# Two attention stages read 64-row operands in place of zero-padded copies, and a third stage's PSUM banks and waits are rearranged

## What is computed

```python
def attn_a(x):                       # 16 heads of 64
    Q, K, V = heads(x @ Wq.T + bq), heads(x @ Wk.T + bk), heads(x @ Wv.T + bv)
    attn = sin(30.0 * (Q @ K.T) / 8)             # no softmax: 2048 x 2048 per head
    return concat(attn @ V) @ Wo.T + bo
def ffn(x):                          # two layers
    for l in range(2):
        q, k, v = split(shift_token(x) @ wqkv[l])          # 8 heads of 64
        q, k = rotary(l2norm(q)), rotary(l2norm(k))
        x = x + softmax(mask(8 * q @ k.T)) @ v @ wo[l]       # window 512: 1 to 5 blocks of 128 keys
        a, g = split(layernorm(shift_token(x)) @ w1[l] + b1[l])
        x = x + (a * gelu(g)) @ w2[l] + b2[l]
    return x
def attn_b(e):                       # two iterations
    for _ in range(2):
        q, k, v = e @ Wq.T, e @ Wk.T, e @ Wv.T             # 16 heads: keys of 16, values of 64
        res = e + softmax(q @ k.T / 4) @ v @ Wp.T
        e = res + relu(res @ W1.T + b1) @ W2.T + b2
    return e
x = x + attn_a(layernorm(x)); x = x + ffn(layernorm(x))
x = x + attn_b(layernorm(x)); x = x + ffn(layernorm(x))
```

## Time and profile before

| | us |
|---|---|
| three runs, median | 35545.85 |
| lowest and highest | 35491.78 and 35622.54 |
| the profiled execution | 35539.34 |
| its span on the slowest core, first to last instruction | 35537.5 |
| TensorE busy on it | 14172.3 (40%) |
| VectorE busy | 8219.3 (23%) |
| ScalarE busy | 6572.5 (18%) |
| mean granted TensorE clock on it | 0.61 of full speed |

### The profile page before, as it was taken

The page is one execution under the profiler, slowest core; times in us unless marked ns, Lnnn a source line. Parts: engine busy times, 40 slices in busy tenths (PEclk is TensorE's granted clock), DMA queues, the critical chain, the costliest instruction groups (busy, mean ns, idle before and its releaser), DMA issues.

```text
span 35537.5 us, 273198 instructions; the slowest of 8 cores (35410.4 to 35537.5 us)
## 1 busy us (share of the span) xinstructions
PE 14172.3 (40%) x81984; PEld 6048.0 (17%) x81984; DVE 8219.3 (23%) x17364; ACT 6572.5 (18%) x8716; POOL 604.9 (2%) x1083
## 2 busy tenths in 40 slices
PE   4555422532532453352333333332253253245235
PEld 1010111211111111121212122221121111111112
DVE  1010033133223213311111111113313322321331
ACT  1313212012002002102323132321201200210210
POOL 0000000000000000000000000000000000000000
PEclk7575555765665675575555555555576576557557
DMA  1010101110120120121010100000111012012012
GB/s 20 0 38 0 31 19 32 35 34 28 37 64 1 47 51 2 37 63 33 13 19 18 39 15 18 13 31 21 32 35 34 27 37 65 1 44 54 2 36 62
DMA packets 618568, 1055.36 MB, mean 30 GB/s; under 512 B 162154, under 2 KB 375395, under 8 KB 617156
## 3 DMA queue, kind: packets, MB, share of 16 engines
q1 hardware_dynamic: 265252, 710.02, 6.0%
q0 software_dynamic: 351904, 327.86, 5.7%
HBM read 987.54 MB, written 301.99 MB: 36 GB/s over the span
## 4 chain that ended last, share of the span: by engine, by line
PE 37%; DVE 21%; ACT 15%; DMA 13%; issue 11%; SPq 1%; DVEq 1%; ACTq 1%; POOL 0%; POOLq 0%
PE ps L901 6%; ACT pool L1204 5%; DMA pool<-zs 5%; PE ps L907 4%; PE ps L951 3%; PE ps L1220 3%; ACT pool L417 3%; DMA pool<-f_w1p 3%; PE ps L402 3%; PE ps L617 3%; ACT pool L755 2%; DMA pool<-xs 2%; DVE pool L748 2%; PE ps L1188 2%; PE ps L794 2%
## 5 line engine op out<-in xcount | busy, mean ns | idle before, releaser
L901 PE MATMUL ps<-pool 128*128 128x512 bf16 x5632 | 2061.2, 533 | 2300.7 <-DMA pool<-f_w1p 1232.7
L951 PE MATMUL ps<-pool 128*128 128x512 bf16 x5632 | 1827.0, 491 | 1411.1 <-DVE pool L974 777.3
L794 PE MATMUL ps<-pool 128*64 128x128 bf16 x4480 | 661.6, 307 | 4260.0 <-ACT pool L786 2249.9
L1204 ACT ACTIVATE pool<-ps 128x2048 bf16<-128x2048 f32 x1024 | 1922.1, 1877 | 2303.6 <-PE ps L1188 2303.5
L253 PE MATMUL ps<-pool 128*128 128x128 bf16 x3328 | 483.6, 299 | 3872.8 <-DMA pool<-zs 1737.7
L1220 PE MATMUL ps<-pool 128*128 128x65 bf16 x16384 | 1063.9, 243 | 2386.9 <-ACT pool L1204 2386.9
L913 ACT ACTIVATE pool<-ps,pool 128x512 f32<-128x512 f32 x704 | 483.8, 687 | 6807.9 <-PE ps L907 6807.8
L917 DVE TENSOR_SCALAR pool<-ps,pool 128x512 f32<-128x512 f32 x704 | 528.4, 751 | 4755.4 <-PE ps L907 4755.4
L907 PE MATMUL ps<-pool 128*128 128x512 bf16 x5632 | 1618.7, 439 | 0.0
L417 ACT ACTIVATE pool<-ps 128x1024 bf16<-128x1024 f32 x1024 | 1048.6, 1024 | 2047.2 <-PE ps L402 2047.2
L755 ACT ACTIVATE pool<-ps,pool 128x640 bf16<-128x640 f32 (+4 forms) x1024 | 744.9, 727 | 3663.7 <-DVE pool L751 3663.7
(11 more groups left out here) (155 smaller groups left out, 17823.8 us busy)
## 6 DMA issues: line engine op xcount, KB each, us to landing
zs<-pool SPq DMA_DIRECT2D x448, 512.0 KB
pool<-zs SPq DMA_DIRECT2D x448, 512.0 KB
pool<-xs SPq DMA_DIRECT2D x192, 512.0 KB
pool<-f_w1p POOLq DMA_DIRECT2D x176, 512.0 KB, 5.9
pool<-zs POOLq DMA_DIRECT2D x312, 256.0 KB, 3.3
xs<-pool SPq DMA_DIRECT2D x96, 512.0 KB
pool<-f_w2p POOLq DMA_DIRECT2D x16, 2816.0 KB, 17.8
pool<-x SPq DMA_DIRECT2D x64, 512.0 KB
```

The costliest lines, as they stand in the source:

```text
L794: first=(ji == 0), last=(ji == nk - 1): e.matmul(PS(5)[0:64, 0:128], vaug[:, 520*kc + 65*h: 520*kc + 65*h + 64], ptb[:, 640*pslot + 128*ji ...
L901: p.op("T", lambda e, kc=kc, tg=tg, abank=abank, w1b=w1b: e.matmul(PS(abank), w1b[:, 256*kc:256*kc+128], hlnFr()[:, kc, 512*tg:512*(tg+1)] ...
L951: last=(ci == nch - 1 and hhalf == 0): e.matmul(PS(bank), ohalf[:, 2048*ci + 128*t: 2048*ci + 128*(t+1)], w2buf[:, 1024*ci + 512*half: 102 ...
L1204: p.op("S", lambda e, eslot=eslot: e.activation(expS[:, 2048*eslot:2048*(eslot+1)], PS(0, 4), AF.Exp), waits=w, inc=sC)
```

## The change

Three parts, in the diff below. In the first attention `kf2`, its zeros, its copies and the wait on them go, and each of the two score matmuls contracts over the 64 partitions on which its head lies: K and Q are read in place, the first head from partitions 0 to 63, the second from 64 to 127. In the local attention `qp2` goes in the same way; the score matmuls of a head read `qpk` and `kpk` on the head's 64 partitions. In the second attention the value slots lie seven, seven and two to a bank; the transposes of the tail, the W1 output and the W2 outputs all go through bank 7; the join on TensorE ahead of W1 is replaced by a wait for VectorE on the first W1 matmul; and the first score matmul of every group but the first waits only for the previous group's last exponential and for VectorE's last copy out of bank 3. The first value matmul of each group also waits for the output projection's last add.

```diff
--- before.py
+++ after.py
@@ -371,43 +371,25 @@
             out=wvo[:].rearrange("p (c k) -> p c k", k=1024),
             in_=io["aWoT"][:].rearrange("(c p) k -> p c k", p=128)),
             waits=[(vC, vC.n)])
-        kf2 = mem.at("a_kf2", [128, 2 * 2048], BF16, mem.offs["a_xt"][0] + 8192)
-        p.op("G", lambda e: e.memset(kf2[64:128, 0:2048], 0.0),
-             waits=[(sC, sC.n), (vC, vC.n)])
-        p.op("G", lambda e: e.memset(kf2[0:64, 2048:4096], 0.0), inc=gC)
-        kzero = gC.n
-        kf2_done, s_last = {}, {}
         sin_done, av_done = {}, {}
         for hp in range(8):
-            wcp = [(vC, vC.n)] if hp == 0 else [(tC, s_last[hp-1])]
-            if hp == 0:
-                wcp.append((gC, kzero))
-            p.op("V", lambda e, hp=hp: e.tensor_copy(
-                kf2[0:64, 0:2048], KF[0:64, 2048*hp:2048*(hp+1)]), waits=wcp)
-            p.op("V", lambda e, hp=hp: e.tensor_copy(
-                kf2[64:128, 2048:4096], KF[64:128, 2048*hp:2048*(hp+1)]), inc=vC)
-            kf2_done[hp] = vC.n
             for qg in range(4):
                 for kc in range(16):
                     par = kc % 2
                     for which in range(2):
                         bank = 2 * par + which
+                        base = 64 * which
                         w = ([(sC, sin_done[(hp, qg, kc - 2)])]
                              if (hp, qg, kc - 2) in sin_done else [])
                         if kc == 0 and which == 0 and (hp, qg) == (0, 0):
                             w = [(sC, sC.n)]
-                        if kc == 0 and which == 0 and qg == 0:
-                            w = list(w) + [(vC, kf2_done[hp])]
-                        p.op("T", lambda e, hp=hp, qg=qg, kc=kc, bank=bank,
-                             which=which: e.matmul(
+                        p.op("T", lambda e, hp=hp, qg=qg, kc=kc, bank=bank, base=base: e.matmul(
                             PS(bank),
-                            kf2[:, 2048*which + 128*kc: 2048*which + 128*(kc+1)],
-                            QF[:, 2048*hp + 512*qg: 2048*hp + 512*(qg+1)],
+                            KF[base:base+64, 2048*hp + 128*kc: 2048*hp + 128*(kc+1)],
+                            QF[base:base+64, 2048*hp + 512*qg: 2048*hp + 512*(qg+1)],
                             start=True, stop=True), waits=w)
                     p.grp("T", tC)
                     smm = tC.n
-                    if qg == 3 and kc == 15:
-                        s_last[hp] = smm
                     slot = par
                     w = [(tC, smm)]
                     if (hp, qg, kc - 2) in av_done:
@@ -502,7 +484,6 @@
     zupd_off = mem.mark() - 2 * 1024 * 4
     scr = mem.seq("f_scr", [128, 1024], F32)
     nrm = mem.seq("f_nrm", [128, 128], F32)
-    qp2 = mem.seq("f_qp2", [128, 2 * 2048], BF16)
     oF = mem.at("f_oF", [128, 4 * 2048], BF16, hF_off)
     hlnF = mem.at("fB_hlnF", [128, 8 * 2048], BF16, hF_off)
     ohalf = mem.at("fB_ohalf", [128, 11 * 2048], BF16, kpk_off)
@@ -521,12 +502,6 @@
     tbr = lambda ti: tabs[:, 1024*ti:1024*(ti+1)].rearrange("p (t k) -> p t k", k=64)
 
     final_phase = dst is not zs and dst is not None
-
-    p.op("G", lambda e: e.memset(qp2[64:128, 0:2048], 0.0),
-         waits=[(sC, sC.n), (vC, vC.n)])
-    p.op("G", lambda e: e.memset(qp2[0:64, 2048:4096], 0.0), inc=gC)
-    qp2_zero = gC.n
-    qp2_war = {0: 0, 1: 0}
 
     for b in range(B_LOC):
         zwr, ln_s = {}, {}
@@ -697,14 +672,6 @@
 
             for h in range(8):
                 hb, hc2 = 64 * (h % 2), h // 2
-                hs = h % 2
-                wcp = [(sC, sC.n), (tC, qp2_war[hs])]
-                if h == 0 and b == 0:
-                    wcp.append((gC, qp2_zero))
-                p.op("V", lambda e, hb=hb, hc2=hc2, hs=hs: e.tensor_copy(
-                    qp2[hb:hb+64, 2048*hs:2048*(hs+1)],
-                    qpk[hb:hb+64, 2048*hc2:2048*(hc2+1)]), waits=wcp, inc=vC)
-                qp2_done = vC.n
                 prev_exp = 0
                 state = {}
                 ptev_hist = {-1: (vC, 0)}
@@ -720,14 +687,12 @@
                     st_ = state[qc] = dict(kcs=kcs, nk=nk, W_=W_, sb0=sb0, pslot=pslot,
                                            stat=stat)
                     w = [(sC, state[qc-2]["exp"])] if qc >= 2 else [(sC, sC.n)]
-                    if qc == 0:
-                        w = list(w) + [(vC, qp2_done)]
                     for ji, kc in enumerate(kcs):
-                        p.op("T", lambda e, hs=hs, hc2=hc2, qc=qc, kc=kc, ji=ji,
+                        p.op("T", lambda e, hb=hb, hc2=hc2, qc=qc, kc=kc, ji=ji,
                              sb0=sb0: e.matmul(
                             PS(sb0, 2)[:, 128*ji:128*(ji+1)],
-                            qp2[:, 2048*hs + 128*qc: 2048*hs + 128*(qc+1)],
-                            kpk[:, 2048*hc2 + 128*kc: 2048*hc2 + 128*(kc+1)],
+                            qpk[hb:hb+64, 2048*hc2 + 128*qc: 2048*hc2 + 128*(qc+1)],
+                            kpk[hb:hb+64, 2048*hc2 + 128*kc: 2048*hc2 + 128*(kc+1)],
                             start=True, stop=True),
                             waits=(w if ji == 0 else []))
                         p.grp("T", tC)
@@ -810,7 +775,6 @@
                     if qc >= 1:
                         emit_tail(qc - 1)
                 emit_tail(NT - 1)
-                qp2_war[hs] = state[NT - 1]["smm"]
             p.join(["T"], [vC, sC])
 
             ldwo = p.dma("G", lambda e, layer=layer: e.dma_start(
@@ -1166,10 +1130,12 @@
             PSF = PS(0, 8)
 
             def AVAP(i):
-                off = 512 * (4 + i // 6) + 65 * (i % 6)
+                off = 512 * (4 + i // 7) + 65 * (i % 7)
                 return PSF[:, off:off + 65]
             av_war = vC.n
             prev_av_last = tC.n
+            exp15_prev = sC.n
+            wp_v_prev = vC.n
             ptv_hist = {}
             bank_tok = {3: (vC, 0), 7: (vC, 0)}
             for ng in range(4):
@@ -1179,8 +1145,12 @@
                     avd = {}
                     exp_done = {}
                     for mg in range(16):
-                        w = ([(sC, exp_done[mg - 1])] if mg >= 1
-                             else [(sC, sC.n), (vC, vC.n)])
+                        if mg >= 1:
+                            w = [(sC, exp_done[mg - 1])]
+                        elif gcg == 0:
+                            w = [(sC, sC.n), (vC, vC.n)]
+                        else:
+                            w = [(sC, exp15_prev), bank_tok[3]]
                         for j in range(4):
                             for s in range(4):
                                 cc = 32 * ((s + j) % 4)
@@ -1212,11 +1182,12 @@
                                 if i == 0:
                                     w = [(sC, exp_done[mg])]
                                     if mg == 0:
-                                        w += [(gC, vones), (vC, av_war)]
+                                        w += [(gC, vones), (vC, av_war),
+                                              (vC, wp_v_prev)]
                                 p.op("T", lambda e, i=i, s=s, qq=qq, mg=mg, cg=cg,
                                      eslot=eslot,
-                                     first=(mg == 0 and i in (0, 6, 12)),
-                                     last=(mg == 15 and i in (5, 11, 15)):
+                                     first=(mg == 0 and i in (0, 7, 14)),
+                                     last=(mg == 15 and i in (6, 13, 15)):
                                      e.matmul(
                                     AVAP(i),
                                     expS[:, 2048*eslot + 512*s + 128*qq:
@@ -1227,8 +1198,9 @@
                         p.grp("T", tC)
                         avd[mg] = tC.n
                     av_last = prev_av_last = avd[15]
+                    exp15_prev = exp_done[15]
                     for jb in range(3):
-                        nsl = (6, 6, 4)[jb]
+                        nsl = (7, 7, 2)[jb]
                         p.op("V", lambda e, jb=jb, nsl=nsl: e.reciprocal(
                             scr[:, 8*jb:8*jb+nsl].rearrange("p (g k) -> p g k", k=1),
                             PSF[:, 512*(4+jb):512*(4+jb) + 65*nsl].rearrange(
@@ -1241,8 +1213,8 @@
                             w = [(vC, rcv), (tC, ptv_hist.get(gcg - 2, 0))]
                         p.op("V", lambda e, i=i, obslot=obslot: e.tensor_scalar_mul(
                             obf[:, obslot + 64*i: obslot + 64*(i+1)],
-                            AVAP(i)[:, 0:64], scr[:, 8*(i//6) + (i % 6):
-                                                  8*(i//6) + (i % 6) + 1]), waits=w)
+                            AVAP(i)[:, 0:64], scr[:, 8*(i//7) + (i % 7):
+                                                  8*(i//7) + (i % 7) + 1]), waits=w)
                     nrmv = vC.n
                     av_war = nrmv
                     for s in range(4):
@@ -1297,7 +1269,7 @@
```

(14 more changed lines are left out.)

## The result

Eight executions of each kernel gave a median of 34877.94 us (34840.6 to 34980.03) for the changed kernel and 35524.63 us (35475.63 to 35622.54) for the one before: ratio 0.982, 95% interval 0.9806 to 0.9835, 647 us faster. The forecast was 34960 us, 1.6% faster; the measured time lies within its range, 28 us above its lower end.

A forecast was written before the change was run, and what follows sets the result against it. No engine is full, so waits from engine to engine bound the kernel. Terms of 405, 37, 9, 72, 15, 33 and 12 us sum to 583 us, giving 34960 us, 1.6% faster, range 34850 to 35260.

The forecast's parts named there:

- The chain: Whole kernel: no engine is full, time is a chain of waits; in the first attention every part is on the path.
- Score pairs, 405 us: First attention: two half-row score matmuls overlap like the value pair, gaining 404.8 us over 1024 steps.
- The gap of 0.17 us: First attention, ahead of each score pair: put down to reshaping the array between kinds of matmul, expected to stay.
- the upper bound: First attention: the score pair also loses the gap in front of it, 174 us more; chance 0.03.
- Copies and zeros, 37 and 9 us: First attention: head-pair boundaries become ordinary steps, 37 us; less TensorE idle at the loop's start, 9 us.
- Local attention, 72 us: Changes of head: without the Q copy the mask add starts 1.28 us earlier, 56 times, 72 us.
- the slower rival: Local attention scores on one half: weight loads exposed, 35405 to 35412 us or 36131; chance 0.06, half of it slower.
- the slack: Local attention: transposes have 3.06 us of slack, hiding a 0.17 us drain after the scores; without it 174 us.
- Second attention, 15 + 33 + 12 us: Earlier scores at 48 group boundaries, 15 us; join ahead of W1, 33 us; scores after a tail, 12 us.
- the added wait: Second attention, first value matmul: waits for an add long past, looked at while the exponential runs; no cost priced.
- The sum: Whole kernel: 405 + 37 + 9 + 72 + 15 + 33 + 12 = 583 us gained.

The follow-up runs named there:

- same_half: Changed kernel with both score matmuls of the first attention on partitions 0 to 63, sharing one half of the rows: 35248.19 us, one execution.
- full_rows: Changed kernel with first-attention score matmuls over all 128 partitions of K and Q in place, no copies or zeros: 35240.49 us, one execution.
- av_wait_last: Changed kernel with the exponential's wait listed last of four at a group's first value matmul in the second attention: 34808.9 us, one execution.
- a_only: Kernel before with the first attention's part of the change alone: 34956.01 us against 35409.23, ratio 0.9869.
- the two last kernels: Changed kernel with scores issued earlier in first and local attention and waits reordered; first-attention scores on half rows 32988.69 us, or zero-padded to 128 rows 32981.63 us.
- pipe_same_half: Changed kernel with the first attention's next scores ahead of the value matmuls and both score matmuls on partitions 0 to 63: 33720.83 us, one execution.
- pipe_full_rows: Changed kernel with first-attention next scores ahead of value matmuls, scores over all 128 partitions in place, no copies or zeros: 33379.64 us, one execution.
- best_half: Changed kernel with scores issued earlier in first and local attention and two wait reorderings, first-attention scores on half rows: 32988.69 us, ratio to before 0.9311.

## Why the prediction was right

**The chain.** No engine is full, and each part of a step lies on the path: `same_half` and `full_rows` show the loops move by the full length of what TensorE loses or gains. The clock lay at 0.50 in that stretch before, and it does after (and at 0.52 in the local attention, as before):

```profile
1000.00:1500.00 500.00, 230.42 (x780) 51.95 (x780) 8.30 (x12) 199.36 (x195) 0.00 (x0) 0.50 0.00 0
```

**Score pairs, 405 us.** Measured 429.2 (3.6 + 425.6). This is the one large term that was mis-sized, low by 24 us: I took the value pair as the model, 0.64 us, and the row-tiled pair takes 0.61. The gap of 0.17 us ahead of it stayed (618.34 to 618.91 is again 0.57 to 0.58 us), so the upper bound did not come about.

**Copies and zeros, 37 and 9 us.** 37.0 us between `before` and `full_rows`, and 2 x 4.83 = 9.7.

**Local attention, 72 us.** Measured 73.6. Five scores on one half take 0.71 us as before, so the slower rival is out. The Trainium skill, "TensorE: Matmul & The Clock Gate", Part 3, "The mechanism", has a weight load overlap a matmul in flight only when the row group differs; the trace disagrees here (0.71 us for five) and in `same_half` (the second starts 0.41 us behind the first). The transposes now start 0.64 us behind the scores in place of 0.51, and the commonest steps stay at 6.03 and 6.87 us, so the 0.13 us lay under the slack as said. The Trainium skill, "TensorEngine Tiling (Array Packing)", "Key Properties", names a drain at a change of tiling mode; the trace agrees with it.

**Second attention, 15 + 33 + 12 us.** Within the four loops lie 48 group changes, 12 joins and 12 tail ends: 15 + 25 + 12 = 52 forecast, 51.4 measured. The sum hides two errors. The group change gained 0.41 us and not 0.31: a satisfied wait that used to stand behind the last one went as well, and the scores start 0.15 us behind the copy that they wait for (16111.55 to 16111.70) in place of 0.25. And the step that failed is the sentence that the added wait "is looked at while the exponential runs". It stands behind the wait for the exponential and costs 0.11 us at each group, 64 times, 7 us; `av_wait_last` takes it away. That the two errors nearly cancel (5 us more, 7 us less) is luck.

**The sum** was 583 us. By the traces' loops 591 us and 18 us outside make 609; the runs say 647, with 586 to 689 by the interval of their ratio. The 38 us between lie within that interval. Of them 26 are the part of the 44 us in the rest of the two traces that no edit explains, and the rest changes by more than that from one chip to another (20478 to 20485 us in the table of `a_only`, 20606 us here).

## What to carry to other kernels

Read which engine's wait ends last in a step before you price a matmul: the same half-row tiles were worth 466 us where the scores stood in the chain and -102 us where they did not, because there full-row matmuls had the higher clock and half-row ones did not. In the two last kernels, where ScalarE set the step, they made no measurable difference. Two matmuls of half the rows run side by side only on different halves; then the pair costs what one does. Count the waits behind the one that comes true last: each costs its own time on the chain, and their order is free to change.

## What the runs showed of the hardware

A TensorE that is busy almost without a break can lie at the lower clock if its scores use half the rows: `pipe_same_half` had it busy for 398.84 of 400 us at a granted clock of 0.50, `pipe_full_rows` for 320.24 at 1.00. The Trainium skill, "TensorE: Matmul & The Clock Gate", in its table "Why this matters for your kernels", says that keeping TensorE continuously busy gets it past the throttle; for the half-row scores of `pipe_same_half` the row disagrees. It is not so for half rows in general, as `best_half` had 0.63.

Waits on semaphores are worked off one after another even when all are true. In the trace's semaphore records those of TensorE ahead of a group's first value matmul start 0.106 us apart, those of ScalarE 0.055 and of VectorE 0.069. The 18 DMA waits of a join come to 1.9 us by that, and taking one join away gained 2.16 us.
